# The recurrent stage of a two-layer decoder: rows of C by DMA, states in PSUM, convolution as matmuls

## The chip, the cores and the metric

The kernel runs on one core of a Trainium2 chip. The metric is the time of one execution on the device in microseconds (us); three runs of the kernel before give 4876.42, 4878.37 and 4889.35 us, and the median, 4878.37, is the time that the change is measured against.

## The reference

The model is a decoder of two layers on a batch of 2 sequences of 1024 tokens with 256 features. Layer 0 begins with a recurrent stage, and only that stage is changed. It runs four blocks one after the other on x; each block normalises, applies the selective scan below and adds the result to x:

```
xz = layer_norm(x) @ in_w;  u, z = split(xz)          # 512 channels each
conv = cb + sum(up[:, k:k+L, :] * cw[:, k] for k in range(4))   # up: u with 3 zeros ahead
u = silu(conv)
dbl = u @ xw                                          # 64 columns for dt, 16 for B, 16 for C
dt = softplus(dbl[..., :64] @ dtw + dtb)
A = -exp(A_log)                                       # 512 channels x 16 states
h = exp(dt * A) * h + (dt * u) * B                    # per step, channel and state
y = sum over the 16 states of h * C
out = ((y + u * D) * silu(z)) @ ow
```

After it come cross-attention, causal attention, a mixture of experts, and layer 1. All of it is done in float32.

## The kernel before, in words

The program has five phases; the recurrent stage (`mamba`) is the first work of the first. It is cut into 16 segments of 512 tokens (4 blocks x 2 sequences x 2 halves of a sequence). A tile has 128 channels on the partitions and 512 tokens in the free dimension, so a segment has 4 channel tiles (m = 0 to 3) and 64 *units*: one unit u is one channel tile and one of the 16 states. The place of a unit in its segment is p = 0 to 63. Of a sequence's two halves the even segment starts from a state of zero and the odd one from the last column of the even one (`carry`).

A unit goes through all engines: ScalarE (ACT) writes the decay exp(dt*A) into a PSUM bank (L638); GpSimd (POOL) writes the drive (dt*u)*B into SBUF (L473); VectorE (DVE) scans the two into the states h (L760), and multiplies h by the row of C (`weigh`, L735); TensorE (PE) adds the product up over the 16 states with an identity matmul (L865). A float32 matmul of 512 columns shows in the trace as two MATMUL passes.

Rows of B come by DMA from a small DRAM buffer, spread over all partitions (256 KB each, one for two units). Rows of C do not: they are split into three bfloat16 parts (L561 to L571 on ACT, L425 and L429 on POOL), and a matmul with a selection matrix (`spread`, L838) lays each into a PSUM bank for two units.

While a segment's 64 units run, the *front* of the next segment f is worked out between them: statistics and normalisation, the turn, the in-projection, the convolution, the x-projection, dt, z. Nothing schedules this at run time. Each engine's order is written out by hand: after the engine's own instruction of the unit at place p comes the front's step that is listed for that p (for example ACT: `tap` at 21, 23, 25, 27; `gate_u` at 28 and 32). An engine works through its list in order, and a step that waits holds up all that stands behind it on that engine, the next decays among it. The front has two PSUM banks, used in turn.

The convolution is done by ACT and DVE. `tap` copies u out of PSUM (L530) and applies the last tap in place (L531); `convolve` on DVE adds the three other taps, two in place in PSUM and one into SBUF (L712, at p = 21, 23, 25, 27). `gate_u` then applies Silu to two tiles at once (L537), with a table load ahead of it and one back to the exponential's table behind it (L542). `gate_z` at p = 60 does the same for z, all four tiles at once (L593).

A decay's bank is one of two: decay u waits until unit u-2 is scanned. DVE's order is scan u, then weigh u-1.

Of the kernel before, what the change touches and what calls it, by code (L numbers as in the profile page):

```python
# [20 lines left out]
P = 128  # L21
# [213 lines left out]
def mamba(sh):  # L235
# [27 lines left out]
    skip_diag = sh.take("p (m q) -> p m q", M * P, m=M)  # L263

# [13 lines left out]
    rest = sh.take(None, BANK)  # L278
    mid0 = sh.take(None, BANK // 2).bitcast(BF16)
    low0 = sh.take(None, BANK // 2).bitcast(BF16)  # L280
    parts = sh.take(None, 2 * BANK // 2).bitcast(BF16).rearrange("p (r s) -> p r s", r=2)
    sel = sh.take("p (n q) -> p n q", NS * P // 2, n=NS).bitcast(BF16)
    RD, RH, RW, RB = 8, 4, 8, 8
    drive = sh.take("p (r s) -> p r s", RD * BANK, r=RD)
    h = sh.take("p (r s) -> p r s", RH * BANK, r=RH)
    hc = sh.take("p (r s) -> p r s", RW * BANK, r=RW)
    b_sb = sh.take("p (r s) -> p r s", RB * BANK, r=RB)
# [6 lines left out]
    b_rows = nc.dram_tensor("mb_b_rows", [2, NS, BANK], F32, kind="Internal").ap()  # L294

    Y, C_BANK, DECAY, FRONT = 0, 2, 4, 6
# [4 lines left out]
    sel_ready, diag_ready = sh.sem("mb_sel_ready"), sh.sem("mb_diag_ready")  # L301
# [3 lines left out]
    taken = [sh.sem(f"mb_taken{r}") for r in range(2)]  # L305
    head_ready, u_copied, tapped, conv = (sh.sem("mb_" + k) for k in ("head_ready", "u_copied", "tapped", "conv"))
    uc_ready, z_ready = sh.sem("mb_uc_ready"), sh.sem("mb_z_ready")
    hi_ready, rest_ready, mid_ready = sh.sem("mb_hi"), sh.sem("mb_rest"), sh.sem("mb_mid")
    low_ready, parts_ready = sh.sem("mb_low"), sh.sem("mb_parts")
    exped, logged, soft = sh.sem("mb_exped"), sh.sem("mb_logged"), sh.sem("mb_soft")  # L310
    dtu_ready = sh.sem("mb_dtu_ready")
    b_stored = sh.sem("mb_b_stored")
    b_in = [sh.sem(f"mb_b_in{r}") for r in range(RB)]
    c_spread = sh.sem("mb_c_spread")
    decay_ready, drive_ready = sh.sem("mb_decay"), sh.sem("mb_drive")
    scanned, weighted, summed = sh.sem("mb_scanned"), sh.sem("mb_weighted"), sh.sem("mb_summed")
# [3 lines left out]
    TURN, UP, XP, DTP, ZP = 0, 2, 6, 7, 11  # L320
    STEPS = 15

    def use(f, step):

        return STEPS * f + 2 * max(f - 2, 0) + step + (2 if f >= 2 and step >= XP else 0)

    def use_out(e, o):

        f = min(e + 2, SEGS)
        return STEPS * f + 2 * e + o + (XP if f < SEGS else 0)  # L330

# [12 lines left out]

    def carries_before(g):

        return (g + 1) // 2 * (UNITS // 2)
# [6 lines left out]
    def sync(eng):  # L354
# [23 lines left out]
        def store_b(f):  # L378
            wait_taken(eng, use(f, XP))
            eng.dma_start(b_rows[f % 2], bc[0:NS, :]).then_inc(b_stored, 16)  # L380

        def load_b(v):
            f, n = v // (UNITS // 2), v % NS
            if v >= RB:
                eng.wait_ge(drive_ready, 2 * (v - RB) + 2)
            eng.wait_ge(b_stored, 16 * (f + 1))
            eng.dma_start(b_sb[:, v % RB, :], b_rows[f % 2, n:n + 1, :].broadcast_to([P, BANK])).then_inc(b_in[v % RB], 16)
# [3 lines left out]
        store_b(0)  # L391
        for v in range(RB):
            load_b(v)
        for g in range(SEGS):
            for j in range(UNITS // 2):
# [7 lines left out]
                if j == UNITS // 2 - RB and g + 1 < SEGS:  # L403
                    store_b(g + 1)
                if v < SEGS * (UNITS // 2):
                    load_b(v)

    def pool(eng):
        eng.memset(eps, EPS).then_inc(eps_ready, 1)
        eng.memset(zeros, 0.0).then_inc(sel_ready, 1)  # L410
        eng.memset(sel, 0.0).then_inc(sel_ready, 1)
        for part in range(3):
            eng.wait_ge(sel_ready, part + 2)
            eng.affine_select(out=sel, in_=sel, compare_op=ALU.not_equal, fill=1.0, base=-32 * part - NS,
                              pattern=[[-1, NS], [0, P]], channel_multiplier=1).then_inc(sel_ready, 1)
# [7 lines left out]
        def rest_of_rows(f):  # L423
            eng.wait_ge(hi_ready, f + 1)
            eng.tensor_tensor(rest[0:32], bc[0:32], parts[0:32, f % 2, :], ALU.subtract).then_inc(rest_ready, 1)  # L425

        def low_of_rows(f):
            eng.wait_ge(mid_ready, f + 1)
            eng.tensor_tensor(low0[0:32], rest[0:32], mid0[0:32], ALU.subtract).then_inc(low_ready, 1)  # L429
# [18 lines left out]
        def dt_times_u(f, m):  # L448
            n = (f * M + m) * SOFT
            eng.wait_ge(uc_ready, 2 * f + m // 2 + 1)  # L450
            eng.wait_ge(soft, n + 4)
            eng.tensor_tensor(dtu[:, f % 2, m, :], dt[:, f % 2, m, :], uc[:, f % 2, m, :], ALU.mult).then_inc(dtu_ready, 1)
# [5 lines left out]

        skip_diagonals(0)
        rest_of_rows(0)  # L460
        low_of_rows(0)
        for m in range(M):
            softplus(0, m)
        for u in range(SEGS * UNITS):
# [7 lines left out]
            eng.wait_ge(b_in[v % RB], 16 * (v // RB + 1))  # L472
            eng.tensor_tensor(drive[:, u % RD, :], dtu[:, g % 2, m, :], b_sb[:, v % RB, :], ALU.mult)\  # L473
# [14 lines left out]
            if f < SEGS:  # L488
                if p == 48:
                    rest_of_rows(f)  # L490
                elif p == 52:
                    low_of_rows(f)
# [12 lines left out]
                elif p == 62 and f % 4 == 0:  # L505
                    eng.wait_ge(c_spread, g * (UNITS // 2) + NS + 4)
                    skip_diagonals(f // 4)

    def scalar(eng):
# [11 lines left out]
        def rows(f, c):  # L521
# [3 lines left out]
                           scale=n_w[:, f // 4, c:c + 1]).then_inc(taken[k % 2], 1)  # L525

        def tap(f, m):
            k = use(f, UP + m)
            eng.wait_ge(front_done, k + 1)
            eng.activation(u_in[:, m, PAD:PAD + BANK], bank(k), ACT.Copy).then_inc(u_copied, 1)  # L530
            eng.activation(bank(k), bank(k), ACT.Identity, bias=cb[:, m:m + 1], scale=cw[:, m, PAD:PAD + 1])\  # L531
                .then_inc(tapped, 1)
# [11 lines left out]
        def next_head(f):  # L544

            eng.wait_ge(u_copied, (f + 1) * M)
# [3 lines left out]
        def rows_of_x(f):  # L550
            k = use(f, XP)
            eng.wait_ge(front_done, k + 1)
            if f:
                eng.wait_ge(b_stored, 16 * f)
                eng.wait_ge(rest_ready, f)
            eng.activation(dt_low[0:R, :], ps[0:R, FRONT + k % 2, :], ACT.Copy)
            eng.activation(bc[0:32, :], ps[R:R + 32, FRONT + k % 2, :], ACT.Copy).then_inc(taken[k % 2], 1)

        def high_rows(f):
            wait_taken(eng, use(f, XP))  # L560
            eng.activation(parts[0:32, f % 2, :], bc[0:32, :], ACT.Copy).then_inc(hi_ready, 1)  # L561

        def mid_rows(f):
            eng.wait_ge(rest_ready, f + 1)
            eng.activation(mid0[0:32, :], rest[0:32, :], ACT.Copy).then_inc(mid_ready, 1)
            eng.wait_ge(mid_ready, f + 1)
            eng.activation(parts[32:64, f % 2, :], mid0[0:32, :], ACT.Copy)

        def low_rows(f):
            eng.wait_ge(low_ready, f + 1)  # L570
            eng.activation(parts[64:96, f % 2, :], low0[0:32, :], ACT.Copy).then_inc(parts_ready, 1)  # L571

        def step(f, m):
# [3 lines left out]
            eng.activation(ey[:, m, :], bank(k), ACT.Abs, bias=dtb[:, m:m + 1]).then_inc(taken[k % 2], 1)  # L577
# [7 lines left out]
        def copy_z(f, m):  # L585
            k = use(f, ZP + m)
            eng.wait_ge(front_done, k + 1)
            eng.activation(sz[:, f % 2, m, :], bank(k), ACT.Copy).then_inc(taken[k % 2], 1)
# [22 lines left out]
        eng.wait_ge(sel_ready, 1)  # L611
        eng.activation(u_in[:, :, 0:PAD], zeros, ACT.Copy).then_inc(head_ready, 1)
        for m in range(M):
            tap(0, m)
# [4 lines left out]
        high_rows(0)  # L619
# [3 lines left out]
        mid_rows(0)  # L623
        low_rows(0)
# [4 lines left out]
        for u in range(SEGS * UNITS):  # L629
# [10 lines left out]
            if p % 2 and u >= 3:  # L640
                v = (u - 3) // 2
                if v // (UNITS // 2) % 2 == 0:
                    first, half = v % NS, v % (UNITS // 2) // NS
                    eng.wait_ge(scanned, 2 * v + 2)
                    eng.activation(carry[:, first, 2 * half:2 * half + 2], h[:, 2 * v % RH:2 * v % RH + 2, BANK - 1], ACT.Copy)\
                        .then_inc(carried, 1)
            if f < SEGS:
# [8 lines left out]
                elif p in (21, 23, 25, 27):  # L656
                    tap(f, (p - 21) // 2)
                elif p == 28:
                    gate_u(f, 0)
                elif p == 32:  # L660
                    gate_u(f, 1)
                elif p == 34:
                    next_head(f)
                elif p == 36 and f % 4 == 0:
                    decays_of(f // 4)
                elif p == 40:
                    rows_of_x(f)
                elif p == 41:
                    high_rows(f)
                elif p in (44, 46, 48, 50):  # L670
                    step(f, (p - 44) // 2)
# [2178 lines left out]
```

## Time and profile before

| | us |
|---|---|
| median of 3 runs | 4878.37 |
| the profiled execution | 4889.27 |
| its span, first to last instruction | 4887.6 |
| first scan to last scan (recurrent stage) | 83.2 to 2130.9 |
| DVE busy in the span | 3347.8 |
| POOL busy in the span | 2261.5 |
| ACT busy in the span | 1997.2 |

The busy time over the span is an average over very different phases; what the change touches is read in the stage's own stretch. A line of the timeline gives the start, the duration, engine, source line and operation, what is written from what, and in brackets the idle time ahead of it with what ended it. A duration runs to the write's acknowledgement, so the next instruction on the same engine may start before it ends.

### The profile page before, as it was taken

The page shows a single profiled execution, that of the slowest core. Times are in us where ns is not written, and L with a number is a line of the kernel's source. Part 1 is how long each engine was busy: PE and PEld are TensorE (multiplying, and loading weights), DVE is VectorE, ACT ScalarE, POOL GpSimd, SP SyncE. Part 2 cuts the span into 40 slices and gives each one's busy share as a digit, 9 for nine tenths or more (in the row PEclk, how much of TensorE's full clock was granted, in tenths as well). Part 3 has the DMA queues.
Part 4 walks back from the last instruction along what each step waited for, and adds up shares of the span by engine and source line. Part 5 has one row for each costly group of instructions (what it writes and reads, how often), then busy time and mean ns, then how long its engine had stood idle before and what let it go on. Part 6 is the DMA issues. An engine that isn't in the chain of part 4 may idle for free. (4 is left out here: it accounts for less than half of the span.)

```text
span 4887.6 us, 50670 instructions
## 1 busy us (share of the span) xinstructions
PE 4027.9 (82%) x16032; PEld 2220.7 (45%) x16032; DVE 3347.8 (68%) x5467; ACT 1997.2 (41%) x3277; POOL 2261.5 (46%) x1890
## 2 busy tenths in 40 slices
PE   5888888888888888849747887999968999967898
PEld 1233333333333333324422325888833444656898
DVE  4999999999999999984576654444445555054433
ACT  4666666666566666522223442111121444322100
POOL 6888888888888888920020111444330111000320
PEclk8999999999999999989977887999987999988899
DMA  2122221222222222210024311000042221000000
GB/s 79 60 66 79 65 71 62 67 79 71 66 67 76 65 71 67 70 48 3 1 89 48 47 19 44 27 26 27 1 109 83 44 52 24 9 15 0 26 18 31
DMA packets 223222, 240.90 MB, mean 49 GB/s; under 512 B 100481, under 2 KB 131516, under 8 KB 222716
## 3 DMA queue, kind: packets, MB, share of 16 engines
q1 hardware_dynamic: 222972, 237.82, 18.0%
q8 instruction: 125, 2.05, 0.2%
q14 instruction: 125, 1.02, 0.1%
HBM read 209.58 MB, written 25.69 MB: 48 GB/s over the span
## 5 line engine op out<-in xcount | busy, mean ns | idle before, releaser
L473 POOL TENSOR_TENSOR arena<-arena 128x512 f32<-128x512 f32 x1024 | 1279.7, 1271 | 289.3 <-DVE arena L760 282.2
L760 DVE TENSOR_TENSOR_SCAN arena<-psum,arena 128x512 f32<-128x512 f32 x1024 | 1271.4, 1242 | 91.1 <-POOL arena L473 50.7
L865 PE MATMUL psum<-arena,base 128*128 128x512 f32 x2048 | 1108.4, 641 | 270.0 <-DVE arena L735 264.4
L638 ACT ACTIVATE psum<-arena 128x512 f32<-128x512 f32 x1024 | 704.5, 689 | 772.9 <-DVE arena L760 769.6
L865 PEld LDWEIGHTS psum<-arena,base 128*128 128x128 f32 x2048 | 355.6, 196 | 909.2 <-DVE arena L735 752.2
L224 POOL TENSOR_TENSOR rounded<-arena,rounded 128x512 fp32r<-128x512 f32 (+2 forms) x181 | 315.3, 1748 | 803.0 <-DVE rounded L220 803.0
L735 DVE TENSOR_TENSOR arena<-arena,psum 128x512 f32<-128x512 f32 x1024 | 673.6, 658 | 0.0
L230 PE MATMUL psum<-rounded 128*128 128x256 f32 (+1 forms) x1728 | 561.4, 325 | 37.4 <-DVE arena L1650 17.9
L231 PE MATMUL psum<-rounded 128*128 128x256 f32 (+1 forms) x1728 | 560.8, 325 | 2.3 <-issue 2.3
L232 PE MATMUL psum<-rounded 128*128 128x256 f32 (+1 forms) x1728 | 559.9, 324 | 0.0
L1119 DVE TENSOR_REDUCE arena<-psum 128x1 f32<-128x512 f32 (+3 forms) x768 | 402.6, 554 | 194.7 <-PE psum L1182 133.3
L1073 POOL TENSOR_SCALAR_AFFINE_SELECT arena<-arena 128x256 f32<-128x256 f32 x256 | 103.9, 407 | 831.6 <-ACT arena L1098 498.5
L1208 PE MATMUL psum<-arena 128*32 128x512 f32 (+7 forms) x1536 | 385.4, 515 | 18.8 <-DVE arena L1147 11.9
L230 PEld LDWEIGHTS psum<-rounded 128*128 128x128 f32 x1728 | 331.7, 192 | 64.4 <-DVE arena L1650 18.0
L231 PEld LDWEIGHTS psum<-rounded 128*128 128x128 f32 x1728 | 331.7, 192 | 28.5 <-issue 3.2
L232 PEld LDWEIGHTS psum<-rounded 128*128 128x128 f32 x1728 | 331.4, 192 | 25.8
L1094 ACT ACTIVATE arena<-psum 128x1024 f32<-128x1024 f32 (+3 forms) x256 | 217.2, 862 | 267.7 <-PE psum L1247 178.8
L1179 PE MATMUL psum<-arena 96*128 96x512 bf16 (+3 forms) x768 | 264.1, 364 | 59.7 <-DVE arena L1119 45.0
L805 PE MATMUL psum<-arena 128*128 128x512 f32 x512 | 259.5, 632 | 53.3 <-DVE arena L712 51.2
L1586 ACT ACTIVATE arena<-psum 128x512 f32<-128x512 f32 x128 | 76.7, 599 | 449.7 <-PE psum L232 449.7
L1658 DVE TENSOR_TENSOR arena<-arena,psum 128x512 f32<-128x512 f32 x128 | 87.9, 687 | 196.7 <-ACT arena L1586 151.0
L1247 PE MATMUL psum<-arena 99*128 99x512 bf16 (+3 forms) x768 | 199.2, 347 | 20.0 <-DMA arena<-arena 10.4
(283 smaller groups left out, 5365.4 us busy)
## 6 DMA issues: line engine op xcount, KB each, us to landing
arena<-mb_b_rows SPq DMA_DIRECT2D x512, 256.0 KB, 3.1
arena<-L_ffn_w SPq DMA_DIRECT2D x34, 512.0 KB, 4.3
arena<-f_parts SPq DMA_DIRECT2D x96, 128.0 KB, 7.0
arena<-l_parts SPq DMA_DIRECT2D x96, 128.0 KB, 6.2
l_v<-arena SPq DMA_DIRECT2D x16, 512.0 KB, 3.5
arena<-l_v SPq DMA_DIRECT2D x32, 256.0 KB, 4.3
f_parts<-arena SPq DMA_DIRECT2D x24, 256.0 KB, 2.4
l_parts<-arena SPq DMA_DIRECT2D x24, 256.0 KB, 2.3
```

Of the source, the lines that this page charges most:

```text
L224: return eng.tensor_tensor(low, src, high.bitcast(F32), ALU.subtract)
L230: eng.matmul(dst, a[0], b[0], start=first, stop=False)
L231: eng.matmul(dst, a[0], b[1], start=False, stop=False)
L232: return eng.matmul(dst, a[1], b[0], start=False, stop=last)
L473: eng.tensor_tensor(drive[:, u % RD, :], dtu[:, g % 2, m, :], b_sb[:, v % RB, :], ALU.mult)\
L638: eng.activation(ps[:, DECAY + u % 2, :], dt[:, g % 2, m, :], ACT.Exp, scale=a_neg[:, g // 4 % 2, m, n:n + 1]).then_inc(decay_ready, 1)
L735: eng.tensor_tensor(hc[:, u % RW, :], h[:, u % RH, :], ps[:, C_BANK + u // 2 % 2, :], ALU.mult).then_inc(weighted, 1)
L760: eng.tensor_tensor_scan(h[:, u % RH, :], ps[:, DECAY + u % 2, :], drive[:, u % RD, :], first, ALU.mult, ALU.add).then_inc(scanned, 1)
L865: mm = eng.matmul(ps[:, Y + u % 2, :], sh.ident, hc[:, u % RW, :], start=False, stop=n == NS - 1)
L1119: eng.tensor_reduce(mx[:, kc, t, h:h + 1], ps[:, A0 + u % 2, 0:w], AX_X, ALU.max)\
L1179: mm = eng.matmul(ps[:, bank, 0:w], qs[i % SLOTS][0:STACK, h, t * P:(t + 1) * P], ks[i % SLOTS][0:STACK, h, kc * BANK:kc * BANK + w], star ...
L1208: mm = eng.matmul(ps[rows, ACC + o % 2, first:BANK], v[:, i % 2, kt, h, :], ex[:, n % RE, k, 0:w], start=kt == 0, stop=kt == 4 * qc + 3)
```

## The change

C's rows are stored beside B's and come by the same DMA, two rows in one transfer (512 KB for two units), into SBUF; the split into three parts, the selection matrix and the spread matmuls go. With the two banks of C the decays have four (ND = 4): the scan writes the states in place over the decays, in PSUM, and the weighing reads the states from PSUM and C from SBUF. Decay u then waits until unit u-4 is *weighed*, and in units that follow an even segment ACT first copies that unit's last state into `carry` (128x1, one for each unit; before 128x2 for two) and waits for the copy. The products' ring shrinks from 8 to 6 buffers and the weighing waits for the matmul that read the buffer.

The convolution becomes four matmuls for each channel tile with diagonal weights (`tap_diag`, made on POOL once a block, 16 multiplications of 128x128), into a front bank of its own step. ACT copies u (one instruction), and Silu reads the convolution from PSUM with the bias, one tile at a time. The places move too:

```diff
-            if u >= 2:
-                eng.wait_ge(scanned, u - 1)
-            eng.activation(ps[:, DECAY + u % 2, :], dt[:, g % 2, m, :], ACT.Exp,
+            if u >= ND:
+                eng.wait_ge(weighted, u - ND + 1)
+                before, m0, n0 = of_unit(u - ND)
+                if before % 2 == 0:
+                    eng.activation(carry[:, n0, m0:m0 + 1], state(u)[:, BANK - 1:BANK], ACT.Copy).then_inc(carried, 1)
+                    eng.wait_ge(carried, before // 2 * UNITS + (u - ND) % UNITS + 1)
+            eng.activation(ps[:, DECAY + u % ND, :], dt[:, g % 2, m, :], ACT.Exp,
...
         def gate_u(f, half):
             for m in (2 * half, 2 * half + 1):
-                wait_taken(eng, use(f, UP + m))
-            eng.activation(uc[:, f % 2, 2 * half:2 * half + 2, :], uc[:, f % 2, 2 * half:2 * half + 2, :], ACT.Silu)\
-                .then_inc(uc_ready, 1)
+                k = use(f, CV + m)
+                eng.wait_ge(front_done, k + 1)
+                eng.activation(uc[:, f % 2, m, :], bank(k), ACT.Silu, bias=cb[:, m:m + 1]).then_inc(taken[k % NF], 1)
             exp_tables()
...
-                elif p in (21, 23, 25, 27):
-                    tap(f, (p - 21) // 2)
-                elif p == 28:
+                elif p in (18, 20, 22, 24):
+                    copy_u(f, (p - 18) // 2)
+                elif p == 29:
                     gate_u(f, 0)
-                elif p == 32:
+                elif p == 34:
                     gate_u(f, 1)
...
         def weigh(u):
-            eng.wait_ge(c_spread, u // 2 + 1)
             eng.wait_ge(scanned, u + 1)
-            eng.tensor_tensor(hc[:, u % RW, :], h[:, u % RH, :], ps[:, C_BANK + u // 2 % 2, :], ALU.mult).then_inc(weighted, 1)
+            if u >= RW:
+                eng.wait_ge(added_up, u - RW + 1)
+            eng.tensor_tensor(hc[:, u % RW, :], state(u), bc_sb[:, u // 2 % RB, 1, :], ALU.mult).then_inc(weighted, 1)
...
-            eng.tensor_tensor_scan(h[:, u % RH, :], ps[:, DECAY + u % 2, :], drive[:, u % RD, :], first,
+            eng.tensor_tensor_scan(state(u), state(u), drive[:, u % RD, :], first,
                                    ALU.mult, ALU.add).then_inc(scanned, 1)
...
-                elif p in (21, 23, 25, 27):
-                    convolve(f, (p - 21) // 2)
...
+        def convolve(f, m):
+            k = use(f, CV + m)
...
+            wait_taken(eng, use(f, UP + m))
+            wait_bank_free(eng, k)
+            for tap in range(KC):
+                mm = eng.matmul(bank(k), tap_diag[:, m, tap, :], u_in[:, m, tap:tap + BANK], start=tap == 0, stop=tap == KC - 1)
+            mm.then_inc(front_done, 1)
...
                 elif p in (15, 17, 19, 21):
                     in_projection(f, 0, (p - 15) // 2)
-                elif p == 33:
+                elif p in (24, 26, 30, 32):
+                    convolve(f, (p - 24) // 2 if p < 28 else (p - 26) // 2)
+                elif p == 36:
                     x_projection(f)
...
+                if p in (12, 13, 14, 15) and f % 4 == 0:
+                    tap_diagonals(f // 4, p - 12)
```

What stands on PE between the last in-projection and the x-projection of a segment, before: L805 is the in-projection, L865 the identity matmuls of the units, L838 the spread of C, L846 the skip path, L814 the x-projection.

```order
L805 MATMUL psum<-arena 128x512
L865 MATMUL psum<-arena,base 128x512 [waits phase0_mb_weighted] x2
L838 MATMUL psum<-arena 128x512 [waits phase0_mb_parts]
L865 MATMUL psum<-arena,base 128x512 [waits phase0_mb_weighted] x2
L838 MATMUL psum<-arena 128x512 [waits phase0_mb_parts]
L865 MATMUL psum<-arena,base 128x512 [waits phase0_mb_weighted] x2
```

And now, in the same place of the same segment: L740 is the in-projection, L805 the identity matmuls, L752 the convolution's matmuls (four a tile), L786 the skip path.

```order
L740 MATMUL psum<-arena 128x512
L805 MATMUL psum<-arena,base 128x512 [waits phase0_mb_weighted] x3
L752 MATMUL psum<-arena 128x512 [waits phase0_mb_taken1,phase0_mb_head_ready,phase0_mb_taps_ready]
L752 MATMUL psum<-arena 128x512 x3
L805 MATMUL psum<-arena,base 128x512 [waits phase0_mb_weighted] x2
L752 MATMUL psum<-arena 128x512 [waits phase0_mb_taken0,phase0_mb_taps_ready]
L752 MATMUL psum<-arena 128x512 x3
L805 MATMUL psum<-arena,base 128x512 [waits phase0_mb_weighted] x4
L752 MATMUL psum<-arena 128x512 [waits phase0_mb_taken1,phase0_mb_taps_ready]
L752 MATMUL psum<-arena 128x512 x3
```

The four convolutions stand behind the identity matmuls of the units at p = 24, 26, 30 and 32, each of which waits for its unit to be weighed.

On ACT the two `gate_u` stand so before (L638 is a decay, L645 the carry, L537 Silu with its table load, L542 the load of the exponential's table):

```order
L638 ACTIVATE psum<-arena 128x512 [waits phase0_mb_scanned]
L537 ACT_TABLE_LOAD [waits phase0_mb_taken0]
L537 ACTIVATE arena<-arena 128x1024 [waits phase0_mb_taken1]
L542 ACT_TABLE_LOAD
L638 ACTIVATE psum<-arena 128x512 [waits phase0_mb_scanned]
```

And now (L608 is a decay, L606 the carry, L522 Silu with its table load, L526 the load of the exponential's table):

```order
L608 ACTIVATE psum<-arena0 128x512 [waits phase0_mb_carried]
L522 ACT_TABLE_LOAD
L522 ACTIVATE arena0<-psum,arena0 128x512 [waits phase0_mb_front_done] x2
L526 ACT_TABLE_LOAD
L606 ACTIVATE arena0<-psum 128x1 [waits phase0_mb_weighted]
L608 ACTIVATE psum<-arena0 128x512 [waits phase0_mb_carried]
```

Silu waited for DVE's convolution; it now waits for `front_done`, which PE counts up, and the next decay stands behind it.

## Rows read from the trace of the kernel before

**Rows 1.** The page: the span of the profiled execution.
```profile
span 4887.6 us, 50670 instructions
```
**Rows 2.** Windows of two segments and the rest: PE, PEld, DVE, ACT, POOL, clock, DMA.
```profile
469.80:600.30 130.50, 108.39 (x257) 42.56 (x256) 127.88 (x156) 79.15 (x120) 109.63 (x90) 0.97 0.25 73
600.30:728.20 127.90, 106.32 (x257) 41.88 (x256) 124.69 (x156) 81.63 (x148) 110.15 (x88) 0.98 0.22 72
2130.90:4887.60 2756.70, 2299.44 (x11979) 1548.99 (x11979) 1333.79 (x2999) 710.57 (x1157) 498.91 (x482) 0.90 0.15 34
```
**Rows 3.** Groups of the stage, 83.2 to 2130.9 us: busy us, mean ns, idle before.
```profile
L473 POOL TENSOR_TENSOR arena<-arena 128x512 f32<-128x512 f32 x1023 | 1278.5, 1271 | 289.3 <-DVE arena L760 282.2 <-issue 7.1
L760 DVE TENSOR_TENSOR_SCAN arena<-psum,arena 128x512 f32<-128x512 f32 x1021 | 1267.6, 1242 | 91.1 <-POOL arena L473 50.7 <-ACT psum L638 39.0
```
**Rows 4.** DVE's timeline in an even segment: start, duration, line, idle ahead.
```profile
619.16 1.21 DVE L760 TENSOR_TENSOR_SCAN arena<-psum,arena 128x512 f32<-128x512 f32 x1
...
639.71 1.21 DVE L760 TENSOR_TENSOR_SCAN arena<-psum,arena 128x512 f32<-128x512 f32 x1
640.85 0.65 DVE L735 TENSOR_TENSOR arena<-arena,psum 128x512 f32<-128x512 f32 x1
...
643.65 1.22 DVE L760 TENSOR_TENSOR_SCAN arena<-psum,arena 128x512 f32<-128x512 f32 x1
...
670.47 1.22 DVE L760 TENSOR_TENSOR_SCAN arena<-psum,arena 128x512 f32<-128x512 f32 x1 [0.59 <-ACT psum L638]
...
723.09 1.22 DVE L760 TENSOR_TENSOR_SCAN arena<-psum,arena 128x512 f32<-128x512 f32 x1 [1.98 <-ACT psum L638]
```
**Rows 5.** DVE's timeline in an odd segment.
```profile
488.38 0.66 DVE L735 TENSOR_TENSOR arena<-arena,psum 128x512 f32<-128x512 f32 x1
488.96 1.27 DVE L760 TENSOR_TENSOR_SCAN arena<-psum,arena 128x512 f32<-128x512 f32 x1
...
510.24 1.26 DVE L760 TENSOR_TENSOR_SCAN arena<-psum,arena 128x512 f32<-128x512 f32 x1
```
**Rows 6.** ACT's timeline in the even segment: carry, and the stretch of gate_z.
```profile
661.23 0.19 ACT L645 ACTIVATE arena<-arena 128x2 f32<-128x2 f32 x1
...
717.14 0.69 ACT L638 ACTIVATE psum<-arena 128x512 f32<-128x512 f32 x1 [0.41 <-DVE arena L760]
717.85 1.28 ACT L593 ACT_TABLE_LOAD   x1
...
722.36 0.69 ACT L638 ACTIVATE psum<-arena 128x512 f32<-128x512 f32 x1
```
**Rows 7.** Groups of the stretch 0 to 2110 us, shapes apart.
```profile
L712 DVE SCALAR_TENSOR_TENSOR psum<-arena,psum 128x512 f32<-128x512 f32 x128 | 96.1, 751 | 13.0 <-ACT psum L531 10.6
L712 DVE SCALAR_TENSOR_TENSOR arena<-arena,psum 128x512 f32<-128x512 f32 x64 | 47.9, 748 | 2.3
L530 ACT ACTIVATE arena<-psum 128x512 f32<-128x512 f32 x64 | 37.1, 580 | 8.4 <-PE psum L805 7.9
L537 ACT ACTIVATE arena<-arena 128x1024 f32<-128x1024 f32 x32 | 33.8, 1057 | 0.4
```
**Rows 8.** The page's DMA issues: count, KB each, us to landing.
```profile
arena<-mb_b_rows SPq DMA_DIRECT2D x512, 256.0 KB, 3.1
```
**Rows 9.** PE's timeline in the odd segment: identity, x-projection, in-projection.
```profile
489.10 1.12 PE L865 MATMUL psum<-arena,base 128*128 128x512 f32 x2 [1.05 <-DVE arena L735]
...
548.00 3.60 PE L814 MATMUL psum<-arena 128*96 128x512 f32 x8
...
573.09 1.88 PE L805 MATMUL psum<-arena 128*128 128x512 f32 x4
```
**Rows 10.** POOL's timeline: small diagonals, first softplus, drives of the odd segment.
```profile
16.69 1.47 POOL L420 TENSOR_TENSOR arena<-base,arena 128x128 f32<-128x128 f32 x4 [6.19 <-DMA arena<-L_attn_A_log]
...
52.35 1.91 POOL L436 TENSOR_SCALAR arena<-arena 128x512 f32<-128x512 f32 x1
...
502.84 16.01 POOL L473 TENSOR_TENSOR arena<-arena 128x512 f32<-128x512 f32 x13
```

More of the change, by code:

```diff
@@ L263, in mamba @@
     skip_diag = sh.take("p (m q) -> p m q", M * P, m=M)
+    tap_diag = sh.take("p (m k q) -> p m k q", M * KC * P, m=M, k=KC)
     PAD = KC - 1
@@ L304, in mamba @@
     front_done = sh.sem("mb_front_done")
[L305 to L309, printed above, removed]
+    taken = [sh.sem(f"mb_taken{r}") for r in range(NF)]
+    head_ready, taps_ready = sh.sem("mb_head_ready"), sh.sem("mb_taps_ready")
@@ L403, in sync @@
                 if j == UNITS // 2 - RB and g + 1 < SEGS:
-                    store_b(g + 1)
+                    store_rows(g + 1)
                 if v < SEGS * (UNITS // 2):
-                    load_b(v)
+                    load_rows(v)
     def pool(eng):
+        eng.wait_ge(*sh.constants)
         eng.memset(eps, EPS).then_inc(eps_ready, 1)
[L410 to L415, printed above, removed]
+        eng.memset(zeros, 0.0).then_inc(zeros_ready, 1)
         def skip_diagonals(i):
@@ L457, in softplus @@
             dt_times_u(f, m)
+        for m in range(M):
+            tap_diagonals(0, m)
         skip_diagonals(0)
-        rest_of_rows(0)
-        low_of_rows(0)
         for m in range(M):
@@ L553, in rows_of_x @@
             if f:
[L554 to L571, printed above, removed]
+                eng.wait_ge(bc_stored, 16 * f)
+            eng.activation(dt_low[0:R, :], ps[0:R, FRONT + k % NF, :], ACT.Copy)
+            eng.activation(bc[0:32, :], ps[R:R + 32, FRONT + k % NF, :], ACT.Copy).then_inc(taken[k % NF], 1)
         def step(f, m):
@@ L587, in copy_z @@
             eng.wait_ge(front_done, k + 1)
-            eng.activation(sz[:, f % 2, m, :], bank(k), ACT.Copy).then_inc(taken[k % 2], 1)
+            eng.activation(sz[:, f % 2, m, :], bank(k), ACT.Copy).then_inc(taken[k % NF], 1)
         def gate_z(f):
@@ L702, in shifts @@
                 .then_inc(shift_ready, 1)
[L704 to L717 removed]
         def gate(g, half, q):
             m = 2 * half + q
[L721 removed]
+            eng.wait_ge(added_up, g * UNITS + (half + 1) * HALF - 1 + q)
             eng.wait_ge(z_ready, g + 1)
@@ L746, in vector @@
         shifts(0)
-        for m in range(M):
-            convolve(0, m)
         for u in range(SEGS * UNITS):
@@ L781, in vector @@
             add_out(SEGS - 1, o)
-        eng.wait_ge(taken[use_out(SEGS - 1, 0) % 2], use_out(SEGS - 1, 0) // 2 + 1)
-        eng.wait_ge(taken[use_out(SEGS - 1, 1) % 2], use_out(SEGS - 1, 1) // 2 + 1)
+        for o in range(2):
+            wait_taken(eng, use_out(SEGS - 1, o))
         eng.memset(rem[:, 0:1], 0.0).then_inc(x_done, 1)
@@ L833, in out_projection @@
             mm.then_inc(front_done, 1)
-        def spread(v):
-            g, n = v // (UNITS // 2), v % NS
-            eng.wait_ge(parts_ready, g + 1)
-            eng.matmul(ps[:, C_BANK + v % 2, :], sel[0:96, n, :], parts[0:96, g % 2, :], start=True, stop=True)\
-                .then_inc(c_spread, 1)
         def skip_path(g, half, q):
@@ L851, in tensor @@
             in_projection(0, 0, m)
+        for m in range(M):
+            convolve(0, m)
         x_projection(0)
@@ L856, in tensor @@
             in_projection(0, 1, m)
-        spread(0)
-        spread(1)
         for u in range(SEGS * UNITS):
@@ L864, in tensor @@
             eng.wait_ge(weighted, u + 1)
-            mm = eng.matmul(ps[:, Y + u % 2, :], sh.ident, hc[:, u % RW, :], start=False, stop=n == NS - 1)
-            if n == NS - 1:
-                mm.then_inc(summed, 1)
-            if p % 2 and u // 2 + 2 < SEGS * (UNITS // 2):
-                spread(u // 2 + 2)
+            eng.matmul(ps[:, Y + u % 2, :], sh.ident, hc[:, u % RW, :], start=False, stop=n == NS - 1).then_inc(added_up, 1)
             if f < SEGS:
```

184 lines of the change are left out of this document (71 added, 113 removed).

## The prediction

> **What bounds the kernel now.** The span is 4887.6 us [rows 1]. I read the windows of the stage first, then the groups of the stage, then the timelines of DVE, ACT and PE in one even and one odd segment. In the windows [rows 2] DVE is busy 127.88 of 130.50 us in an odd segment and 124.69 of 127.90 in an even one; ACT has 79 to 82, POOL 110, PE's matmuls 106 to 108. So DVE is the bound of the stage, and all after 2130.9 us is not touched. The scan's group [rows 3] says how little DVE waits: 39.0 us for decays, spread over the segments, and 50.7 us for the very first drive; POOL waits 282.2 us for scans to free its ring of drives, so it isn't the bound either. Inside a segment [rows 4] twelve units take 619.16 to 639.71, so an even unit is T = 1.71 us; an odd one [rows 5] takes 21.28/12 = 1.77. One tile's convolution costs DVE 643.65 - 639.71 - 1.71 = 2.23. The two waits with weight in a segment stand behind ACT's `gate_u` (0.59 at 670.47) and `gate_z` (1.98 at 723.09), where ACT is busy with tables and Silu and its next decay is late [rows 4, 6].
>
> **What goes.** Four convolutions a segment leave DVE: 4 x 2.23 = 8.9 us. The idle time on ACT goes with them and is worked out anew below; it was about 3.4 us in an even segment (0.59, 1.98, the rest in tenths) and 2.3 in an odd one. Spread matmuls and the split of C free PE, ACT and POOL, none of which is the bound.
>
> **What does not matter.** A scan that writes PSUM in place is not in the trace. The nearest rows are the convolution's own instructions, which read and write one bank in place: 751 ns into PSUM, 748 into SBUF [rows 7]. I take 3 ns (3 us in all). The other end is the spread between the two kinds of scan, 0.06 us a unit [rows 4, 5]: 1024 x 0.06 = 61 us; nothing shows a PSUM write that is faster, so the low end is 0. The Trainium skill (Perfetto Trace Analysis, "Optimizing Scalar/DVE Operations") gives DVE's overhead for an access as about 60 ns on SBUF and 125 on PSUM; as an estimate by that page 1024 scans would pay 67 us. By that rule it is a rival (below); the rows of this trace do not agree with it. C's transfer is 512 KB where 256 KB land in 3.1 us [rows 8]: 3.1 to 6.2 us. A pair's load is issued once the pair eight before it is weighed, and POOL can use it only seven units (12 us) later, so it is hidden.
>
> **What comes: ACT waits for PE.** ACT runs ahead of DVE by at most four units: decay u starts when unit u-4 is weighed, and scan u is wanted two units after that. What ACT may be held up by beyond a decay is thus some 2.4 us. `gate_u` at ACT's p = 29 waits for the convolution that PE starts behind the identity matmul of p = 26, so behind the weighing of unit 26, while ACT has passed decay 29 when unit 25 was weighed. The wait is built into the places. Durations: weighing u ends at scan u+1 plus 1.80 (1.14 and 0.66 [rows 4]); PE starts 0.06 later [rows 5, 9], an identity matmul takes 0.96 from idle and 0.86 in a queue, four float32 matmuls 3.60 to their end and 3.43 to the next one's start, two of them 1.88 [rows 9]; a copy out of PSUM holds ACT 0.48 (0.58 [rows 7], the next starts 0.10 earlier); Silu of 512 columns is 1.06 less half of the difference to gate_z's 2048 (4.51 in all, less two loads of 1.29: 1.93), so about 0.62 (bounds 0.58 for a plain copy and 1.06 for twice the columns: 13 us in all at most); a table load 1.29, the carry 0.22 (0.19 and the wait), a decay 0.69 [rows 6]; 0.04 from engine to engine.
>
> An even segment, `gate_u` of m = 0 and 1, time zero at scan 25. Unit 24 is weighed at 1.80; PE's identity 24 ends at 2.82, convolution 0 holds PE to 6.25, identities 25 and 26 to 7.96, convolution 1 is done at 11.56. ACT has waited since decay 29 with its table loaded; Silu, load, carry and decay 30 put scan 30 at 11.60 + 0.62 + 1.29 + 0.22 + 0.69 + 0.03 = 14.45. It is wanted at 5T = 8.56. Stall: 5.9 us.
>
> `gate_u` of m = 2 and 3, zero at the late scan 30. Unit 30 is weighed at 3.51, its identity matmul ends at 4.53, convolution 2 leaves PE at 7.96; identity 31, skip path and identity 32 (0.86 each) end at 10.54, convolution 3 at 14.14. Scan 35 comes at 14.14 + 0.04 + 0.62 + 1.29 + 0.22 + 0.69 + 0.03 = 17.03; wanted at 5T plus two gates of 0.59 and 0.4 that the second gate waits for PE: 10.2. Stall: 6.8 us, and the 0.4.
>
> The copies of u, at ACT's 18 to 24 against PE's 15 to 21: from scan 15, unit 15 is weighed at 3.51, in-projection done at 6.41, copy, carry and decay put scan 19 at 7.87, wanted at 6.85: 1.0 us; the second copy hides behind it, the third pays again. 2.0 us. `gate_z`: decay 61 starts 0.34 after scan 59, then 0.63, 4.51 and 0.91, so scan 62 at 6.42 against 5.14: 1.3 us (the same sum for the kernel before gives 2.0; the row says 1.98). Steps of dt: 0.1. Together 16.5 us. An odd segment has T = 1.77 and no carry: 5.4, 6.6, 0.3, 1.4 and 0.7, together 14.3.
>
> **The sum.** Even segment: 16.5 - 8.9 - 3.4 = +4.2; odd: 14.3 - 8.9 - 2.3 = +3.1. Eight even and seven odd ones prepare a next segment: 33.6 + 21.7 = 55 us. POOL's new diagonals, 16 x 0.37 = 5.9 us [rows 10], come at p = 12 to 15 of three odd segments, where POOL has work between the drives: drive 19 starts at 502.84 and ends at 504.1, its scan at 488.96 + 10 x 1.77 = 506.7, so 2.6 of the 5.9 are hidden and 3.3 are paid, 10 us for three. The start: POOL's first softplus stood behind the split of C at 52.35 [rows 10]; now it waits for the front alone, and starts at about 48 (an estimate: the front gets 13.7 us of convolutions on PE, of which some 8 us take the place of DVE's): -4. In all +61 us. The profiled execution took 4889.3 (its span and 1.7 around it), and would take 4950; it lay 10.9 above the median of the runs. The forecast for the median is 4878.4 + 61 = 4939, 1.3% slower.
>
> **Rivals.**
> - *The gain comes through.* If ACT's steps are ready when ACT reaches them, only gate_z stalls: even 1.3 - 8.9 - 3.4 = -11.0, odd 0.7 - 8.9 - 2.3 = -10.5, in all -162 with the same +6 elsewhere: 4722. For it: DVE is full, and its list gets 7% shorter. Against: the order itself; it decides at 8.9 + 3 us of stall a segment, and one `gate_u` alone costs half of that. Chance 0.06.
> - *The wait is there, but without a queue on PE.* Convolution 1 right behind identity 26, convolution 3 right behind identity 32: 4.1 and 5.2 us, no stall of the copies: even 10.7 - 12.3, odd 9.3 - 11.2: -26 + 6, so 4858. Against: PE has 5.1 us of work in two units of 3.4 there. Chance 0.12.
> - *A PSUM write costs the scan 0.06 us.* +61 more: 5000. Against: 751 and 748. Chance 0.10. Between this and the forecast lies a slower Silu or a PE clock that falls further below the 0.97 and 0.98 of the windows [rows 2] (nearly all of it at 2.4 GHz); 3% of nine us is 0.3 a stall.
> - *C's rows come late.* With loads that double and queue, POOL would wait and DVE behind it; it takes more than 12 us to landing, four times the row. Chance 0.03, 5 us or more a segment: above 5000.
>
> **How the numbers follow.** The forecast has 0.69, with its own range of 4895 to 4975: the sum of the stalls is a difference of two large numbers, and an error of 2 us a segment is 30 us. What a measurement of this kernel can't tell from no change is 0.3%, 15 us: 4864 to 4893. Faster: the first rival and half of the second, 0.13. Same: the other half and the low tail of the forecast, 0.10. Slower 0.77. The range for 8 in 10 reaches to the second rival below and to most of the third above: 4860 to 4990.
>
> **What would show it.** Right: the scan's idle time on decays rises from 39 to over 200 us, in two stretches of 5 to 7 us in each segment, behind the Silu of `gate_u`, and that Silu is released by the convolution's matmul; DVE's busy share falls to about 90%. An even segment takes 132 us and an odd one 133. The scan lasts as long as before (1.21 and 1.27). Wrong: segments of 118 to 120 us, a scan of 1.27 and more in even segments, waits of POOL on the rows' DMA, or Silu that finds its convolution done.

## The result and the profile after

The changed kernel takes 4961.84 us (median of 4 runs, 4949.28 to 4971.77), the kernel before 4877.4 in the same comparison: a ratio of 1.0165, 95% interval 1.0138 to 1.0193, so slower. A second comparison gave 4964.09 us and 1.0186 (1.0160 to 1.0211). The forecast was 4939, its own range 4895 to 4975.

The profiled execution of after took 4949.28 us, the shortest of its four; that of before (4889.27) was among the longest of its own. So the stage is compared, not the spans. Its last scan, in the profile of before (L760) and of after (L698):

```profile
2134.89 1.26 DVE L760 TENSOR_TENSOR_SCAN arena<-psum,arena 128x512 f32<-128x512 f32 x1
2221.94 1.28 DVE L698 TENSOR_TENSOR_SCAN psum<-psum,arena 128x512 f32<-128x512 f32 x1
```

It starts 87 us later (the 2130.9 given as the stage's end ahead of the prediction is two units early; no step rests on it). The medians differ by 84.

The windows of the third and the fourth segment of after, an even and an odd one (columns as in [rows 2]):

```profile
348.80:482.70 133.90, 114.58 (x256) 45.38 (x256) 115.96 (x144) 83.00 (x172) 106.54 (x84) 0.96 0.46 126
482.70:620.00 137.30, 116.30 (x257) 45.64 (x256) 120.12 (x144) 74.07 (x114) 112.97 (x104) 0.96 0.50 134
```

DVE lost some 8 to 9 us of work (115.96 against 124.69, 120.12 against 127.88) and yet the segments are longer: it waits 18 and 17 us in them, where it waited 3. From first scan to first scan, the 15 segments that prepare another took 133.6 to 134.9 (even) and 135.3 to 137.3 (odd), 91 us more than before in all; the first scan of the stage starts 4 us earlier. In the sixteenth segment, which prepares none, the last scan starts 115.6 us behind the first, before 115.3.

The page's groups of the scan, the drive and the weighing, which answer to [rows 3], and its row of the DMA for [rows 8]:

```profile
L698 DVE TENSOR_TENSOR_SCAN psum<-psum,arena 128x512 f32<-128x512 f32 x1024 | 1278.9, 1249 | 303.0 <-ACT psum L608 232.4
L461 POOL TENSOR_TENSOR arena<-arena 128x512 f32<-128x512 f32 x1024 | 1279.7, 1270 | 417.0 <-DVE psum L698 411.2
...
L678 DVE TENSOR_TENSOR arena<-psum,arena 128x512 f32<-128x512 f32 x1024 | 689.2, 673 | 0.0
...
arena<-mb_bc_rows SPq DMA_DIRECT2D x512, 512.0 KB, 4.8
```

The scan's wait for decays rose from 39.0 to 232.4 us; its own duration went from 1242 to 1249 ns. The groups of Silu and of the copies of u on ACT, and of the gates on DVE, over the stage:

```profile
L522 ACT ACTIVATE arena<-psum,arena 128x512 f32<-128x512 f32 x64 | 44.0, 687 | 222.3 <-PE psum L752 222.3
L665 DVE TENSOR_TENSOR arena<-psum,arena 128x512 f32<-128x512 f32 x62 | 42.1, 679 | 22.9 <-PE psum L805 22.9
...
L516 ACT ACTIVATE arena<-psum 128x512 f32<-128x512 f32 x64 | 38.3, 598 | 145.7 <-PE psum L740 145.7
```

ACT, which had no wait of weight for PE, waits 222 us for the convolutions and 146 for the in-projections. How that reaches DVE is read in one even segment on three timelines. First DVE (scan L698, gate L665), from the first `gate_u` to the late scan behind the second:

```profile
406.19 0.68 DVE L678 TENSOR_TENSOR arena<-psum,arena 128x512 f32<-128x512 f32 x1
412.72 1.23 DVE L698 TENSOR_TENSOR_SCAN psum<-psum,arena 128x512 f32<-128x512 f32 x1 [5.86 <-ACT psum L608]
...
423.46 0.69 DVE L665 TENSOR_TENSOR arena<-psum,arena 128x512 f32<-128x512 f32 x1 [2.04 <-PE psum L805]
...
431.54 1.23 DVE L698 TENSOR_TENSOR_SCAN psum<-psum,arena 128x512 f32<-128x512 f32 x1 [6.79 <-ACT psum L608]
```

Then ACT (L522 Silu and its table, L526 the table back, L606 carry, L608 decay):

```profile
402.66 1.28 ACT L522 ACT_TABLE_LOAD   x1
404.65 0.69 ACT L522 ACTIVATE arena<-psum,arena 128x512 f32<-128x512 f32 x1 [0.71 <-PE psum L752]
409.80 0.69 ACT L522 ACTIVATE arena<-psum,arena 128x512 f32<-128x512 f32 x1 [4.46 <-PE psum L752]
410.50 1.28 ACT L526 ACT_TABLE_LOAD   x1
411.80 0.17 ACT L606 ACTIVATE arena<-psum 128x1 f32<-128x1 f32 x1
412.00 0.69 ACT L608 ACTIVATE psum<-arena 128x512 f32<-128x512 f32 x1
...
422.60 0.69 ACT L522 ACTIVATE arena<-psum,arena 128x512 f32<-128x512 f32 x1 [4.12 <-PE psum L752]
428.61 0.69 ACT L522 ACTIVATE arena<-psum,arena 128x512 f32<-128x512 f32 x1 [5.32 <-PE psum L752]
```

And PE (L805 identity matmuls, L752 convolution, L786 skip path):

```profile
401.01 3.60 PE L752 MATMUL psum<-arena 128*128 128x512 f32 x8
404.45 1.88 PE L805 MATMUL psum<-arena,base 128*128 128x512 f32 x4
406.16 3.60 PE L752 MATMUL psum<-arena 128*128 128x512 f32 x8
409.60 1.88 PE L805 MATMUL psum<-arena,base 128*128 128x512 f32 x4
414.59 1.13 PE L805 MATMUL psum<-arena,base 128*128 128x512 f32 x2 [3.11 <-DVE arena L678]
416.31 1.95 PE L805 MATMUL psum<-arena,base 128*128 128x512 f32 x2 [0.59 <-DVE arena L678]
418.04 4.52 PE L752 MATMUL psum<-arena 128*128 128x512 f32 x8
```

Convolution 1 ends at 409.76, Silu starts at 409.80, the decay at 412.00, the scan at 412.72, 5.86 late. What the prediction did not have stands at the end: while DVE is held up PE has nothing to add up and is idle for 3.11 us, and shortly after its work has come back it is slow. The window of that stretch has the granted clock (the last but two of the row) at 0.54, about the lower of its two levels, 1.2 GHz:

```profile
416.30:420.00 3.70, 3.69 (x5) 1.63 (x6) 3.70 (x5) 2.13 (x3) 2.80 (x3) 0.54 0.55 149
```

An identity matmul takes 1.95 in place of 1.12, convolution 2 takes 4.52 in place of 3.60. The odd segment has the same picture: 5.42, a gate wait of 1.86, 6.59.

The two large stalls are the same in every segment of their kind; the clock's loss is not. Behind the second stall of this segment PE is idle for 3.12 us and the clock is 0.54 again from 433.30 to 437.00, at no cost to DVE. Over the 15 segments the gate waits 0.9 to 2.35 us, 22.9 in all, so the 2.04 shown is among the longest. In six of the seven segments whose gate waits 1.2 or less, the scan at p = 42, behind the x-projection, waits another 0.5 to 1.2, 5 in all.

### The profile page after: what moved, and what is told of

Same layout as the page of the kernel before. It is cut to its first block and busy times, and to the rows that moved or that the text cites. A ratio compares the mean times of both kernels' runs of the same rounds, so it can differ in the third digit from the quotient of the medians.

```text
span 4947.6 us, 50701 instructions
## 1 busy us (share of the span) xinstructions
PE 4121.3 (83%) x16032; PEld 2265.6 (46%) x16032; DVE 3217.0 (65%) x5275; ACT 1967.1 (40%) x3437; POOL 2241.6 (45%) x1918
## 3 DMA queue, kind: packets, MB, share of 16 engines
q14 instruction: 124, 1.02, 0.1%
## 5 line engine op out<-in xcount | busy, mean ns | idle before, releaser
L698 DVE TENSOR_TENSOR_SCAN psum<-psum,arena 128x512 f32<-128x512 f32 x1024 | 1278.9, 1249 | 303.0 <-ACT psum L608 232.4
L805 PE MATMUL psum<-arena,base 128*128 128x512 f32 x2048 | 1142.2, 662 | 338.9 <-DVE arena L678 338.5
L805 PEld LDWEIGHTS psum<-arena,base 128*128 128x128 f32 x2048 | 352.5, 199 | 1027.5 <-DVE arena L678 877.7
L608 ACT ACTIVATE psum<-arena 128x512 f32<-128x512 f32 x1024 | 698.4, 689 | 245.8 <-DVE arena L678 225.6
L678 DVE TENSOR_TENSOR arena<-psum,arena 128x512 f32<-128x512 f32 x1024 | 689.2, 673 | 0.0
L740 PE MATMUL psum<-arena 128*128 128x512 f32 x512 | 242.9, 599 | 1.5 <-ACT arena L510 1.1
L752 PE MATMUL psum<-arena 128*128 128x512 f32 x512 | 238.0, 609 | 0.0
L1596 DVE TENSOR_TENSOR arena<-arena,psum 128x512 f32<-128x512 f32 x128 | 88.0, 687 | 189.9 <-ACT arena L1524 145.7
```

What stands on the lines that cost most here:

```text
L608: eng.activation(ps[:, DECAY + u % ND, :], dt[:, g % 2, m, :], ACT.Exp, scale=a_neg[:, g // 4 % 2, m, n:n + 1]).then_inc(decay_ready, 1)
L678: eng.tensor_tensor(hc[:, u % RW, :], state(u), bc_sb[:, u // 2 % RB, 1, :], ALU.mult).then_inc(weighted, 1)
L698: eng.tensor_tensor_scan(state(u), state(u), drive[:, u % RD, :], first, ALU.mult, ALU.add).then_inc(scanned, 1)
L805: eng.matmul(ps[:, Y + u % 2, :], sh.ident, hc[:, u % RW, :], start=False, stop=n == NS - 1).then_inc(added_up, 1)
```

## The experiments

Each was run beside the kernel before on the same chip: spread, one_tap, conv_dve and half_dma where that took 4891.9 us (8 runs), the other four where it took 4881.49 (13 runs). The theory: ACT waits for PE because its steps stand too few places behind PE's, and ACT runs only some three places ahead of the scan. The rivals: the states in PSUM, C's transfers, or the amount of work on PE cost the time.

### The places alone: spread

```diff
-                elif p == 29:
+                elif p == 32:
                     gate_u(f, 0)
-                elif p == 34:
+                elif p == 41:
                     gate_u(f, 1)
...
-                elif p in (24, 26, 30, 32):
+                elif p in (23, 25, 32, 34):
                     convolve(...)
```

The other steps of the front move with them (the copies of u at 19 to 25 behind in-projections at 14 to 20, x-projection at 39, dt and z up to 62).

> Same instructions as in the changed kernel, other places: on ACT the copies of u stand five places behind PE's in-projection, the two gate_u (places 32 and 41) seven and more behind their convolutions (23, 25, 32, 34), and the steps of dt and z five places behind PE's. Theory (ACT waits for PE because it runs only some three places ahead of DVE's scan): the stalls of 5.9 and 6.8 us go, those of the copies too, gate_z's 1.2 stays; an even segment takes some 117 to 120 us in place of 134, an odd one 120 to 123 in place of 136, the whole 4720 (4700 to 4780), faster than the kernel before. Rival A (the time is lost to the scan into PSUM or to a slower clock on PE whatever the places): segments stay above 128 us, 4900 or more. Rival B (PE, with 115 us of work a segment, becomes the bound): segments of 125 to 128 us, the waits of DVE end with PE's identity matmuls, about 4850.

Measured: 4744.34 us (4722.26 to 4754.09), ratio 0.9695 (0.9659 to 0.9731): faster than both kernels. Segments took 118.6 (all even ones) and 120.8 to 122.8 us. The groups of scan, gate and Silu over the stage:

```profile
L698 DVE TENSOR_TENSOR_SCAN psum<-psum,arena 128x512 f32<-128x512 f32 x1024 | 1276.7, 1247 | 100.7 <-POOL arena L461 66.2 <-ACT psum L608 28.4 <-issue 5.4
...
L665 DVE TENSOR_TENSOR arena<-psum,arena 128x512 f32<-128x512 f32 x64 | 43.1, 674 | 0.8 <-PE psum L805 0.8
...
L522 ACT ACTIVATE arena<-psum,arena 128x512 f32<-128x512 f32 x64 | 40.7, 684 | 7.6 <-PE psum L752 7.2
```

The same instructions at other places: Silu's wait for PE fell from 222 to 7 us, the scan's for ACT from 232 to 28, while the scan itself lasts as long (1247 ns). So it is the places. PE is not the bound with the shorter segments either: DVE's gates wait 0.8 us for it in the whole stage, and the windows of two segments show a granted clock of 0.97 and 1.00:

```profile
342.00:461.00 119.00, 109.14 (x257) 45.93 (x256) 115.87 (x142) 81.92 (x163) 107.43 (x91) 0.97 0.57 153
461.00:582.00 121.00, 106.89 (x253) 43.96 (x252) 118.46 (x144) 75.21 (x122) 110.76 (x97) 1.00 0.52 140
```

### One place alone: gate_later

```diff
-                elif p == 29:
+                elif p == 31:
                     gate_u(f, 0)
```

> The changed kernel with the first gate_u on ACT at place 31 in place of 29, nothing else. Theory (a step on ACT has the time of each place by which it stands further behind PE's): the first stall shrinks by two units of 1.72 us, from 5.9 to about 2.4; the second gate_u keeps its place, and its stall is 6.1 to 6.8; with a shorter idle time on PE part of the clock loss goes. Some 4 to 6 us a segment, 60 to 90 in all: 4875 to 4905. Rival (the sum of table loads, Silu and PE's work sets the stall, not the distance): unchanged, 4950 to 4970.

Measured: 4882.67 us (4873.72 to 4898.26, 10 runs), ratio 1.0007 (0.9988 to 1.0026); the changed kernel beside it took 4964.09. One number takes away 81 us, the whole loss. DVE's timeline of the even segment has the first stall at 2.43 and the second at 6.44, and no wait of the gate:

```profile
403.71 1.23 DVE L698 TENSOR_TENSOR_SCAN psum<-psum,arena 128x512 f32<-128x512 f32 x1 [2.43 <-ACT psum L608]
416.59 1.23 DVE L698 TENSOR_TENSOR_SCAN psum<-psum,arena 128x512 f32<-128x512 f32 x1 [6.44 <-ACT psum L608]
```

Over the 15 segments the first stall is 3.4 to 3.6 us shorter, 52 in all, and the second 0.3, 5 in all; the gate waits of 23 us are gone. In the segment shown PE now has work through the shorter stall, and its granted clock is 1.00 from 402 to 413 us.

### The yardstick of that chip: again

> The changed kernel once more, as a yardstick for the three below on the same chip: 1.0165 times the kernel before, the stage 87 us longer than before's, segments of 134 and 136 us.

Measured: 4964.09 us (4961.87 to 4971.20), 1.0186 (1.0160 to 1.0211); segments of 133.9 to 134.7 and 135.3 to 137.3 us.

### The clock: keep_busy

```diff
+                elif p in (28, 33):
+                    for i in range(3):
+                        eng.matmul(ps[:, Y + u % 2, :], idle_w, w_in[...], start=False, stop=False)
```

`idle_w` holds zeros.

> The changed kernel with three matmuls of zero weights (they add zero to the bank of the products) behind the identity matmuls of places 28 and 33, where PE waits 3.1 us for DVE. Theory (PE's granted clock falls to 0.55 after its idle time, which makes an identity matmul 0.8 and the third convolution 0.9 us longer and the gate wait 2.04 us): the clock stays at 1.00 in that stretch, the gate's wait falls to about 0.4, the third convolution takes 3.60; each segment is 1.6 to 2.0 us shorter, 24 to 30 in all, about 4935. Rival (the clock falls for another reason, or the added matmuls stand in the way of PE's next work): the clock is as low as before, and the time is that of the changed kernel or longer.

Measured: 4936.92 us (4930.68 to 4940.84), ratio 1.0124 (1.0098 to 1.0150), 27 us less than the changed kernel. PE's timeline (L818 the added matmuls, L808 identity, L754 convolution) has no slow stretch left between the two stalls, and the gate on DVE waits 0.35:

```profile
407.04 2.74 PE L818 MATMUL psum<-arena 128*128 128x512 f32 x6
410.32 1.12 PE L808 MATMUL psum<-arena,base 128*128 128x512 f32 x2 [0.54 <-DVE arena L680]
412.03 1.12 PE L808 MATMUL psum<-arena,base 128*128 128x512 f32 x2 [0.59 <-DVE arena L680]
413.00 3.60 PE L754 MATMUL psum<-arena 128*128 128x512 f32 x8
```

```profile
408.45 1.23 DVE L700 TENSOR_TENSOR_SCAN psum<-psum,arena 128x512 f32<-128x512 f32 x1 [5.86 <-ACT psum L610]
417.49 0.69 DVE L667 TENSOR_TENSOR arena<-psum,arena 128x512 f32<-128x512 f32 x1 [0.35 <-PE psum L808]
425.56 1.23 DVE L700 TENSOR_TENSOR_SCAN psum<-psum,arena 128x512 f32<-128x512 f32 x1 [6.79 <-ACT psum L610]
```

The window of that stretch has a granted clock of 1.00:

```profile
410.00:416.40 6.40, 5.49 (x12) 2.30 (x13) 6.40 (x9) 3.05 (x6) 4.83 (x4) 1.00 0.38 125
```

Even segments take 132.2 us (one 133.1), odd ones 133.7 (135.5 with the tap diagonals): the 132 and 133 of the prediction. The gate waits 0.35 in every even and 0.17 in every odd one, the scan at p = 42 never, and the two large stalls are those of after. The last scan starts at 2194.14, 28 us before that of after (in again, on the same chip, it is 2222.03). More work on PE made the kernel faster, because the added work lies in PE's idle time and keeps the clock.

### PE's queue: conv_early

```diff
-                elif p in (24, 26, 30, 32):
+                elif p in (23, 26, 30, 32):
                     convolve(...)
```

> The changed kernel with the first convolution on PE at place 23 in place of 24, nothing else, so that the second finds no queue of identity matmuls ahead of it. Theory: the second convolution ends 1.7 us earlier, the first stall falls from 5.9 to 4.1 us, the rest stays: 15 x 1.7 = 26 us less than the changed kernel, about 4936. Rival (PE has no queue to speak of): within 5 us of the changed kernel.

Measured: 4950.71 us (4939.19 to 4960.71), 1.0147 (1.0115 to 1.0179): 13 us less than the changed kernel, half of what was expected; the intervals of the two ratios overlap, so the verdict rests on the rows. The first stall is 5.00, not 4.1, and PE's timeline says why:

```profile
397.56 3.60 PE L752 MATMUL psum<-arena 128*128 128x512 f32 x8
400.99 2.74 PE L805 MATMUL psum<-arena,base 128*128 128x512 f32 x6
403.57 3.60 PE L752 MATMUL psum<-arena 128*128 128x512 f32 x8
```

Convolution 0 starts one unit (1.72) earlier, but the queue does not vanish: three identity matmuls stand between the two instead of two, 0.86 more. The gain is 1.72 - 0.86 = 0.86, and 5.86 - 5.00 is that. The expectation forgot that the place gained is filled by one more unit. In odd segments the first stall is 4.50 or 3.93 for 5.42, but in three of them the gate waits 3.1 us; the stage ends at 2211.94 for 2222.03 in again, 10 us earlier.

### A quarter of the convolution: one_tap

```diff
-            for tap in range(KC):
-                mm = eng.matmul(..., start=tap == 0, stop=tap == KC - 1)
+            for tap in range(KC - 1, KC):
+                mm = eng.matmul(..., start=True, stop=True)
```

> The changed kernel with one of the four tap matmuls of each convolution; three taps of the convolution are left out. Theory: each convolution holds PE 0.9 us in place of 3.6; the stall behind the first gate_u falls from 5.9 to about 1.4 us, that behind the second from 6.8 to about 2, and with PE's shorter gaps the clock loss too: some 10 us a segment, the whole about 4815 (4790 to 4840). Rival (ACT's Silu and its table loads, or DVE in PSUM, set the stalls): stalls stay near 6 us, 4940 or more.

Measured: 4831.54 us (4828.49 to 4833.88), ratio 0.9883 (0.9862 to 0.9905). The first stall is 1.57 (1.4 expected), the second 4.08 (2 expected) in the even segment shown, and 2.75 to 4.64 over all:

```profile
381.78 1.23 DVE L698 TENSOR_TENSOR_SCAN psum<-psum,arena 128x512 f32<-128x512 f32 x1 [1.57 <-ACT psum L608]
395.73 1.23 DVE L698 TENSOR_TENSOR_SCAN psum<-psum,arena 128x512 f32<-128x512 f32 x1 [4.08 <-ACT psum L608]
```

PE's work does set the stalls. The second is larger because the clock loss stayed, against that part of the expectation. PE is idle for 2.26 us behind the first stall, then runs slowly until the gates (the granted clock is 0.50 from 383.65 to 387.20), and the work queues up to the last convolution at 391.74:

```profile
383.65 3.79 PE L805 MATMUL psum<-arena,base 128*128 128x512 f32 x4 [2.26 <-DVE arena L678]
387.23 1.92 PE L752 MATMUL psum<-arena 128*128 128x512 f32 x2
```

### The rest of the change alone: conv_dve

```diff
-                elif p in (24, 26, 30, 32):
-                    convolve(f, (p - 24) // 2 if p < 28 else (p - 26) // 2)
+                elif p in (21, 23, 25, 27):
+                    convolve(f, (p - 21) // 2)
```

The removed lines are PE's, the added ones DVE's; ACT's `tap` and `gate_u` and their places are again those of the kernel before. C by DMA and the states in PSUM stay.

> The other half of the change alone: C's rows by DMA, four banks of decays, states in PSUM; the convolution as in the kernel before (last tap on ACT, three on DVE), its places as before. Theory: this half costs DVE only some 5 ns a unit and gives ACT more lead, so the wait behind gate_u (0.6 us) goes and part of gate_z's (2.0 to 1.3), the start gains some 4 us: about 4850 (4830 to 4875). Rival (C's transfer or the PSUM states are what costs): 4900 or more, with a scan of 1.27 us or more in even segments or waits on the rows' DMA.

Measured: 4859.01 us (4842.64 to 4869.19, 5 runs), 0.9936 (0.9911 to 0.9962). This half gains a little, though its scan too takes 1247 ns: even segments take 126.3 to 127.2, odd ones 128.8. Two parts of the expectation failed: the wait behind `gate_u` did not go (0.45 for 0.59 in an even segment; `gate_z`'s did fall from 1.98 to 1.24), and the first scan starts 9 us earlier than before, not 4. So the loss is the convolution's alone: by the ratios it costs 1.0165 - 0.9936 = 0.0229, some 112 us, at the change's places, and gains 0.9936 - 0.9695 = 0.0241, some 118 us, at those of spread.

### C's bytes: half_dma

```diff
-            rows = bc_rows[f % 2].rearrange("(k n) s -> n k s", k=2)[n:n + 1]
-            eng.dma_start(bc_sb[:, v % RB], rows.broadcast_to([P, 2, BANK]))
+            eng.dma_start(bc_sb[:, v % RB, 0, :], bc_rows[f % 2, n:n + 1, :].broadcast_to([P, BANK]))
```

> The changed kernel with B's row alone in each transfer (256 KB in place of 512); the weighing reads B's row where C's belongs. Theory: the transfer is hidden, the time stays: 4955 to 4970. Rival (C's traffic slows DVE or POOL or holds up drives): 4940 or less, and a scan or a product that is shorter than 1249 and 1270 ns.

Measured: 4951.12 us (4944.56 to 4964.60), 1.0127 (1.0097 to 1.0157). That is 4 us under the range expected. Its interval overlaps that of the changed kernel's first comparison and lies just under that of the second, so the rows decide, and what would show a cost is not there: the scan takes 1248 ns, its wait for decays is 231.5, the segments (133.6 to 134.9, 135.4 to 137.2) are those of after, and the last scan starts at 2221.75 for 2221.94.

## Why the prediction was right, and what it mis-sized

- *DVE bounds the stage, and 8.9 us a segment leave it.* Right: busy 116 (even) and 120 (odd) against 125 and 128, and spread shows that the gain can be had. The sign given for it, a busy share of about 90%, was loosely worked out: some 116 us in the forecast 132 are 88%, and the windows show 87%.
- *ACT waits for PE, and DVE for ACT.* Right in place and size: 5.86 and 6.79 for 5.9 and 6.8 (even), 5.42 and 6.59 for 5.4 and 6.6 (odd), 2.0 for the copies (0.18, 0.92, 0.92), 1.24 for 1.3 behind `gate_z`. One Silu holds ACT for 0.70 (409.80 to 410.50) where 0.62 was taken.
- *The gate's wait of 0.4 and 0.3.* This is the term that was mis-sized: 2.04 and 1.86. The prediction priced PE's matmuls behind the stall at the durations of [rows 9], taken where PE had been working; here PE comes out of 3 us of idle time and a clock of 0.54 follows. Over the stage the gates wait 19 us more than in keep_busy and the scans at p = 42 another 5; keep_busy's stage is 28 us shorter in all, its median 27. The prediction named a lower clock only as 3% of nine us, 0.3 a stall: it took the mean of the windows for what holds right behind an idle stretch. With the clock held, keep_busy's gates wait 0.35 and 0.17, which the sum had. The Trainium skill (TensorE: Matmul & The Clock Gate, "HAM oscillation — how this bites in real kernels") has a kernel whose matmuls wait for data at each tile and start each one at half the clock again; this trace agrees in kind, with its 0.54, though in the segment shown the first identity matmul behind the idle stretch still ran at 1.00.
- *PSUM writes are nearly free.* Right: 7 ns a scan (3 taken), and 15 ns more for the weighing (673 for 658), which now reads the state from PSUM and C from SBUF. From scan to scan it is some 5 ns (1.717 for 1.7125 in an even segment), about 5 us in all. The rival of 61 us fell. The Trainium skill (Perfetto Trace Analysis, "Optimizing Scalar/DVE Operations") gives 60 and 125 ns for an access to SBUF and PSUM; the spacing of units in this trace does not show that difference.
- *C's transfer is hidden.* Right: 4.8 us to landing, no wait of POOL for rows, and half the bytes change nothing that the rows show.
- *POOL's tap diagonals, 10 us.* Too dear: the three segments that have them (137.0 to 137.3) grew by 6.5 to 6.8, the other odd ones by 4.8 to 5.4, some 1.5 each; in keep_busy, where the clock does not blur it, the difference is 1.8. That is 5 in all.
- *The start, -4.* Right: the first softplus on POOL starts at 47.51 for 52.35 [rows 10], the first scan at 78.81 for 83.24.
- *The first rival (the gain comes through, 4722)* is what spread shows once the places allow it, 4744 (its ratio of 0.9695 makes 4730 of before's 4878); the second (no queue on PE) was tried in part by conv_early, which removed half of the queue's price only.

Together: 61 predicted, 87 found. In keep_busy the stage ends 59 us later than before, so without the clock's loss the sum is out by 2 only; the clock is the other 28. That the 59 is so near the 61 is in part luck: the diagonals were 5 too dear, the spacing of units 2 too cheap, and the rest in tenths a segment. Two small slips stand in its sums: the odd segment's terms make 14.4, not 14.3 (under 1 us in all), and the first rival with half of the second makes 0.12, not 0.13.

## What to carry to other kernels

When work moves from the bounding engine to another, each step that waits for it must stand so many places behind it that the wait is covered by the lead its engine really has; here that lead is some three places. With PE's second convolution at p = 26, `gate_u` at 29 cost 5.9 us a segment and at 31 still 2.4; in spread, with five places for the copies and seven for `gate_u`, little is left. One number in a table of places decided between 1.7% slower and no loss, the whole table between 1.7% slower and 3% faster. A stall on one engine makes others idle, and PE's next matmuls after such idle time are not to be priced at the durations of its busy stretches.

## What was not expected of the hardware

In the segment shown PE's granted clock was 1.00 in the idle 3 us and in the first identity matmul behind it, and 0.54 in the 3.7 us from 416.30, 1.7 us after work had come back; then it was 1.00 again until the next idle stretch. The place is not fixed: in again the same segment has 0.90 from 413 to 416 us and 0.65 from 416 to 420, with matmuls back at 415.39; convolution 2 keeps its 3.60, the gate waits 1.19, and the scan at p = 42 another 1.17. In one_tap 2.26 us of idle time were followed by matmuls of 1.92 us in place of 1.02. Six matmuls of zero weights in the idle time, twice 2.74 us of PE a segment, bought some 1.8 us a segment (27 us over 15).

A low clock by itself says little: from 880 to 2130 us conv_dve has a mean of 0.94, the kernel before 0.97 and after 0.95, and conv_dve is the fastest of the three. In this kernel it cost time where DVE's waits end with PE's work, at the gates directly and at the scans through ACT.
